# Part products stacked as 128 + 16 rows instead of 72 + 72, and the work around them put in another order, in the first of four attention-like layers

## The reference, cut to what matters

```
a = layer_norm(audio_kv)
Q, K, V = x @ Wq.T, a @ Wk.T, a @ Wv.T          # 16 heads of 16
scores  = where(mask, Q K^T / 4, -inf)
x       = x + tanh(gate) * (softmax(scores) V) @ Wo.T
```

## Time and profile before

| | |
|---|---|
| median of 3 timed runs | 1302.26 us |
| lowest and highest | 1301.91 and 1302.64 us |
| span of the profiled execution | 1301.2 us |
| mean granted clock of TensorE in it | 0.970 |
| instructions | 17916 |

### The profile page before, as it was taken

How to read it: one execution, slowest core, us unless ns; L and a number is a source line. 1 busy time by engine, 2 the same in 40 slices (tenths; PEclk the granted TensorE clock), 3 DMA queues, 4 the chain that set the end, 5 groups by cost and what they waited for, 6 DMA issues and landing times.

```text
span 1301.2 us, 17916 instructions
## 1 busy us (share of the span) xinstructions
PE 1222.6 (94%) x6064; PEld 859.9 (66%) x6064; DVE 792.9 (61%) x2354; ACT 537.2 (41%) x1233; POOL 216.2 (17%) x429
## 2 busy tenths in 40 slices
PE   6789989999998879999998899999999999999998
PEld 4467655556464434444433788888888888888887
DVE  4445438778675157787875666666656666666530
ACT  3145343444444315545555343434333434343432
POOL 3023025242434020112101100000000000000000
PEclk9689799999999879999999999999999999999999
DMA  7434741110202455515426903030303030500000
GB/s 226 141 114 136 222 155 64 57 64 35 81 26 93 135 177 183 159 73 164 139 83 198 312 1 130 1 130 1 130 1 130 1 131 1 195 1 1 1 9 25
DMA packets 100650, 127.58 MB, mean 98 GB/s; under 512 B 6736, under 2 KB 78576, under 8 KB 98320
## 3 DMA queue, kind: packets, MB, share of 16 engines
q1 hardware_dynamic: 99936, 126.14, 29.6%
q10 hardware_dynamic: 624, 0.30, 0.1%
HBM read 79.33 MB, written 46.79 MB: 97 GB/s over the span
## 4 chain that ended last, share of the span: by engine, by line
PE 79%; DMA 6%; DVE 4%; SPq 3%; ACT 3%; POOL 2%; issue 2%; ACTq 0%; POOLq 0%; DVEq 0%
PE J L2464 8%; PE J L2484 8%; PE TT L2472 8%; PE TT L2448 4%; PE S L2438 4%; PE OO L2438 4%; PE OO L1091 4%; PE OO L1088 4%; PE J L324 2%; PE J L1357 2%; PE OO L2705 2%; PE J L1091 2%; PE S L1327 2%; PE S L648 2%; PE J L333 2%
## 5 line engine op out<-in xcount | busy, mean ns | idle before, releaser
L2542 ACT ACTIVATE PT<-TT 128x512 f32<-128x512 f32 x128 | 76.4, 597 | 279.9 <-PE TT L2448 279.9
L2577 POOL COPY On<-probs 128x8 f32<-128x8 f32 x128 | 29.2, 228 | 470.0 <-DVE probs L2612 440.7
L2623 DVE TENSOR_SCALAR QK<-J,cols 128x256 f32<-128x256 f32 x126 | 61.0, 484 | 68.5 <-PE J L2464 68.5
L2612 DVE TENSOR_SCALAR probs<-probs,inv 128x257 f32<-128x257 f32 x256 | 79.0, 351 | 4.5
L2448 PE MATMUL TT<-ident,probs 128*128 128x128 f32 x512 | 76.9, 273 | 2.6 <-DVE probs L2612 2.6
L2448 PEld LDWEIGHTS TT<-ident,probs 128*128 128x128 f32 x512 | 63.8, 141 | 16.4 <-DVE probs L2612 3.8
L2618 DVE COPY km<-TT 128x256 f32<-128x256 f32 x128 | 54.2, 423 | 30.6 <-PE TT L2472 30.3
L1091 PE MATMUL OO<-ctxT,weights_a 128*128 128x512 f32 x136 | 66.4, 610 | 6.2 <-SPq L308 3.5
L1088 PE MATMUL OO<-weights_a,ctxT 128*128 128x512 f32 x136 | 65.9, 607 | 6.6 <-ACT weights_a L1102 3.4
L2331 DVE TENSOR_TENSOR_SCAN early<-km,early 128x256 f32<-128x256 f32 x64 | 64.3, 1044 | 10.9 <-ACT early L2102 10.1
L2484 PE MATMUL J<-early,km 128*128 128x256 f32 x256 | 65.8, 379 | 0.3 <-DVE km L2618 0.3
(11 more groups left out here) (414 smaller groups left out, 2711.7 us busy)
## 6 DMA issues: line engine op xcount, KB each, us to landing
wide_keys<-weights_a SPq DMA_DIRECT2D x64, 256.0 KB, 2.1
wide_values<-weights_a SPq DMA_DIRECT2D x56, 256.0 KB, 2.0
query_parts<-weights_a SPq DMA_DIRECT2D x48, 192.0 KB, 2.9
weights_a<-wide_keys SPq DMA_DIRECT2D x16, 512.0 KB, 7.3
weights_a<-wide_values SPq DMA_DIRECT2D x16, 512.0 KB, 8.4
early<-wide_keys SPq DMA_DIRECT2D x16, 512.0 KB, 7.8
early<-wide_values SPq DMA_DIRECT2D x16, 512.0 KB, 9.1
weights_a<-key_parts SPq DMA_DIRECT2D x16, 288.0 KB
```

Source lines behind the costliest of these rows:

```text
L2542: act.activation(PT[:, n % 2, :], T0[:, :], ACT.Copy).then_inc(pt3_ready, 1)
L2612: ins = dve.tensor_scalar(P_[n % 2][:, qt, :], P_[n % 2][:, qt, :], inv[:, qt, n % 32:n % 32 + 1], None, ALU.mult)
```

## The change

- The 144 rows lie as 128 + 16. Rows are ordered by query part `a`, feature, key part `c`: 48 rows for `a` = 0, 48 for `a` = 1, 32 for `a` = 2 with `c` below 2 fill the first tile; the 16 rows of the two lowest parts (`a` = `c` = 2) are the second tile, with the 3 rows of the maxima below them (`REST0`).
- A fill multiplies the first tile alone: two matmuls in place of four. The lowest part product is thus missing from the maxima, but not from the scores that the exponential sees: `transposed_scores` still uses both tiles.
- The queries are kept as two stores of 192 KB per batch, not six; both sides are repeated on reading. A step's rows now come in eight DMAs (48, 48, 32 and 16 rows for the keys, the same for the queries), each with the 16 features as outermost dimension of the source.
- The rows of steps 1 to 3 are asked for ahead of SP's loop; those of step n + 3 in step n, chunk 2. Batch 3 is prepared in step 1 (before in step 2), its statistics and root in step 0, and the values of batch 1 in step 0 (before in step 1).
- Ahead of the loop there is only unit 0; units 1 to 7 stand between the fills, at chunks -13, -11, -9, -7, -6, -5 and -3.

```diff
+        FEATS0 = 2 * HALF0
+        REST0 = FEATS0
+        TOPS0 = [PARTS, PARTS, PARTS - 1]
+        ROWS0 = [0, PARTS * FEATS0, 2 * PARTS * FEATS0]
...
+        FIRST_AT = [-13, -11, -9, -7, -6, -5, -3]
...
-            return n // 2 + 2 if n >= 0 and n % 2 == 0 and n // 2 + 2 < B else None
+            return n + 2 if 0 <= n < B - 2 else None
...
             for s in range(2):
-                for c in range(PARTS):
-                    sp.dma_start(query_parts0[b, s, :, c].rearrange("a p n -> p a n"),
-                                 parts0["q"][:, :, s * S:(s + 1) * S]).then_inc(query0_kept, 16)
+                sp.dma_start(query_parts0[b, :, s].rearrange("a p n -> p a n"),
+                             parts0["q"][:, :, s * S:(s + 1) * S]).then_inc(query0_kept, 16)
...
+        def feature_rows(parts, first):
+            return parts.rearrange("c s (d h) n -> (s d) c (h n)", d=HALF0)[:, :, first * S:(first + HEADS_AT) * S]
...
-            for s in range(2):
-                sp.dma_start(k_rows0[m % 4][0:ROWS0, s, :, :],
-                             key_parts0[b, s].rearrange("c (d h) n -> (c d) (h n)", d=HALF0)[:, here]
-                             .unsqueeze(0).to_broadcast([PARTS, PARTS * HALF0, n_here]))\
+            keys = feature_rows(key_parts0[b], first)
+            for a, top in enumerate(TOPS0):
+                sp.dma_start(k_rows0[m % 4][ROWS0[a]:ROWS0[a] + top * FEATS0, 0, :, :], keys[:, 0:top, :])\
                     .then_inc(rows0_landed[m % 4], 16)
+            sp.dma_start(k_rows0[m % 4][0:REST0, 1, :, :], keys[:, 2, :]).then_inc(rows0_landed[m % 4], 16)
...
+                sp.dma_start(q_rows0[m % 4][ROWS0[a]:ROWS0[a] + top * FEATS0, 0, :, :],
+                             queries[:, a:a + 1, :].to_broadcast([FEATS0, top, HEADS_AT * S]))\
...
             spread0(sp, 0)
+            keep_keys0(sp, 1)
             spread0(sp, 1)
-            keep_keys0(sp, 1)
             keep_queries0(sp, 1)
+            spread0(sp, 2)
+            spread0(sp, 3)
...
+                if 1 <= n <= STEPS0 - 4 and i == 2:
+                    spread0(sp, n + 3)
...
-                        for s in range(2):
-                            mm = pe.matmul((S0, S1)[n % 2][:, qt * S:(qt + 1) * S],
-                                           q_rows0[m % 4][0:ROWS0, s, f, qt * P:(qt + 1) * P],
-                                           k_rows0[m % 4][0:ROWS0, s, f, :], start=(s == 0), stop=(s == 1))
+                        mm = pe.matmul((S0, S1)[n % 2][:, qt * S:(qt + 1) * S],
+                                       q_rows0[m % 4][:, 0, f, qt * P:(qt + 1) * P],
+                                       k_rows0[m % 4][:, 0, f, :], start=True, stop=True)
...
-                            top = ROWS0 + (PARTS if s == 1 else 0)
+                            top = (P, REST0 + PARTS)[s]
...
-                for u in range(FIRST - 1):
...
+                first_unit(0)
...
                         if i == 0:
                             pe.wait_ge(max0_rows_ready, n + 1)
+                            if prepared(n - 1) is not None:
+                                pe.wait_ge(queries0_ready, following)
                             flip_x(following, O1)
...
-                    if i == 7 and n >= 0 and n % 2 == 1 and b + 1 < B:
+                    if i == 7 and n == 0:
+                        pe.wait_ge(h0_ready, 2)
+                        values(1, J0)
+                    if i == 7 and n >= 3 and n % 2 == 1 and b + 1 < B:
...
-                    if at == -1:
-                        u = FIRST + at
-                        pe.wait_ge(ahead_copied, u - 1)
-                        project_ahead(pe, (J1, O0)[u % 2], u)
+                    if at in FIRST_AT:
+                        first_unit(1 + FIRST_AT.index(at))
...
-                    if n in (-1, 1) and i == 0:
-                        root((n + 5) // 2 + 1)
+                    if n in (-1, 0) and i == 0:
+                        root(n + 4)
```

More of the change, by code:

```diff
@@ L514, in build @@
                   for n, i in (("q", 14336), ("k", 15104))}
-        key_parts0 = nc.dram_tensor("key_parts_0", [B, 2, PARTS, P, S], BF16).ap()
-        query_parts0 = nc.dram_tensor("query_parts_0", [B, 2, PARTS, PARTS, P, S], BF16).ap()
+        key_parts0 = nc.dram_tensor("key_parts_0", [B, PARTS, 2, P, S], BF16).ap()
+        query_parts0 = nc.dram_tensor("query_parts_0", [B, PARTS, 2, P, S], BF16).ap()
         RING0 = [T0, T1, O0]
+        FIRST_AT = [-13, -11, -9, -7, -6, -5, -3]
         def fill_of(at):
@@ L530, in keep_keys0 @@
             for s in range(2):
-                sp.dma_start(key_parts0[b, s].rearrange("c p n -> p c n"),
+                sp.dma_start(key_parts0[b, :, s].rearrange("c p n -> p c n"),
                              parts0["k"][:, :, s * S:(s + 1) * S]).then_inc(key0_kept, 16)
@@ L550, in spread_keys0 @@
                 sp.wait_ge(st0_done, CHUNKS0 * (m - 3))
-            here = slice(first * S, (first + HEADS_AT) * S)
-            n_here = HEADS_AT * S
             sp.wait_ge(key0_kept, 16 * 2 * (b + 1))
-            for s in range(2):
-                sp.dma_start(k_rows0[m % 4][0:ROWS0, s, :, :],
-                             key_parts0[b, s].rearrange("c (d h) n -> (c d) (h n)", d=HALF0)[:, here]
-                             .unsqueeze(0).to_broadcast([PARTS, PARTS * HALF0, n_here]))\
+            keys = feature_rows(key_parts0[b], first)
+            for a, top in enumerate(TOPS0):
+                sp.dma_start(k_rows0[m % 4][ROWS0[a]:ROWS0[a] + top * FEATS0, 0, :, :], keys[:, 0:top, :])\
                     .then_inc(rows0_landed[m % 4], 16)
+            sp.dma_start(k_rows0[m % 4][0:REST0, 1, :, :], keys[:, 2, :]).then_inc(rows0_landed[m % 4], 16)
         def spread_queries0(sp, m):
             b, first = m // 2, m % 2 * HEADS_AT
-            here = slice(first * S, (first + HEADS_AT) * S)
-            sp.wait_ge(query0_kept, 16 * 2 * PARTS * (b + 1))
-            for s in range(2):
-                sp.dma_start(q_rows0[m % 4][0:ROWS0, s, :, :],
-                             query_parts0[b, s].rearrange("a c (d h) n -> (a c d) (h n)", d=HALF0)[:, here])\
+            sp.wait_ge(query0_kept, 16 * 2 * (b + 1))
+            queries = feature_rows(query_parts0[b], first)
+            for a, top in enumerate(TOPS0):
+                sp.dma_start(q_rows0[m % 4][ROWS0[a]:ROWS0[a] + top * FEATS0, 0, :, :],
+                             queries[:, a:a + 1, :].to_broadcast([FEATS0, top, HEADS_AT * S]))\
                     .then_inc(rows0_landed[m % 4], 16)
+            sp.dma_start(q_rows0[m % 4][0:REST0, 1, :, :], queries[:, 2, :]).then_inc(rows0_landed[m % 4], 16)
         def split0(eng, n, ready, done_sem, turn, step_sem, at):
@@ L602, in stacked0_sp @@
                     store_first(sp, i)
[L603 to L613, removed]
+                if prepared(n) is not None and i == 4:
+                    keep_keys0(sp, prepared(n))
+                if prepared(n - 1) is not None and i == 1:
+                    keep_queries0(sp, prepared(n - 1))
+                if 1 <= n <= STEPS0 - 4 and i == 2:
+                    spread0(sp, n + 3)
                 if n == 4 and i == 2:
                     sp.wait_ge(key0_kept, 16 * 2 * B)
-                    sp.wait_ge(query0_kept, 16 * 2 * PARTS * B)
+                    sp.wait_ge(query0_kept, 16 * 2 * B)
                     load_values()
@@ L642, in fill @@
                     if f == 0:
-                        pe.wait_ge(rows0_landed[m % 4], 16 * 4 * (m // 4 + 1))
+                        pe.wait_ge(rows0_landed[m % 4], 16 * 8 * (m // 4 + 1))
                     if n >= 2:
@@ L726, in pe_program, with first_unit @@
                 pe.wait_ge(loaded["quarter"], 16)
-                for u in range(FIRST - 1):
+                def first_unit(u):
                     if u == 1:
@@ L771, in pe_program @@
                         if n == 1:
-                            pe.wait_ge(h0_ready, 2)
+                            pe.wait_ge(values0_ready, 2)
+                        elif n == 2:
+                            pe.wait_ge(ot0_ready, 1)
                         elif n % 2 == 1:
@@ L826, in fetch_queries @@
                         act.wait_ge(queries0_split, b)
-                        act.wait_ge(query0_kept, 16 * 2 * PARTS * b)
+                        act.wait_ge(query0_kept, 16 * 2 * b)
                     act.activation(exact0["q"], bank_[:, :], ACT.Copy, scale=DIM0 ** -0.5)
@@ L871, in act_program @@
                 act.wait_ge(mask_ready, 4)
-                for u in range(FIRST - 1):
-                    copy_first(act, (J1, O0)[u % 2], u)
+                copy_first(act, (J1, O0)[0], 0)
                 for at in range(-LEAD0, LAST0):
                     n, i = at // CHUNKS0, at % CHUNKS0
-                    if at == 0:
-                        copy_first(act, (J1, O0)[(FIRST + at - 1) % 2], FIRST + at - 1)
+                    if at - 1 in FIRST_AT:
+                        u = 1 + FIRST_AT.index(at - 1)
```

(11 more changed lines are left out.)

11 lines of the change are left out of this document (1 added, 10 removed).

## The result

The changed kernel takes 1284.34 us (median of four runs, 1283.18 to 1286.75) against 1302.45 (1301.91 to 1302.78) for the kernel before, measured beside it: a ratio of 0.9854, 95% interval [0.9825, 0.9884]. It is faster, and the time lies inside the range, but 18 us were gained where 38 were forecast. The profiled execution took 1286.75 us, its span 1284.9; 1.85 us lie around the span, where I had taken 1.0.

What follows compares the result with a forecast made beforehand. PE was taken as the bound from chunk 0, with waits and half clock. Of 37.9 us saved, 10.7 came from the head, 11.0 from matmuls, 10.6 from clock, 5.7 from waits: 1264 us, range 1254 to 1285.

Steps and rivals of the forecast that it cites:

- Part 1: Loop from chunk 0: 100 fill matmuls fewer at 0.11 us each, 11.0 us off, leaving 83.1 us; transposed scores unchanged.
- rival C: Head and loop: clock stays at half, partly because transposed scores use tiles of 16 or 19 rows; 1351 us, chance 0.03.
- the signs that I listed: New profile: first fill about 31, chunk 0 near 51, fills 0.22, DMA share near 1, clock 0.9 or more, end near 148.
- the signs of being wrong: First fill after 36, `L663` waiting on the maxima's DMA in several steps, or clock 0.5 for over some 20 us of loop.
- Part 2: Row spreads: features outermost bring them near the loads' pace, 3.6 us for a step's rows, against 15.1 at the old pace.
- Part 3: Head, step by step: first fill at 30.7 instead of 40.45 us, chunk 0 at 51 instead of 61.71, bounds 48 and 58.
- Part 4: Loop: 3 us of waits and 3 us for half clock added to 83.1 give 89.1; traffic costed at nothing.
- A: Loop: waits move to the maxima's DMA, 2.4 us more in each of four steps plus half clock; 1281 us, chance 0.18.
- D: Layer's end: the next layer's loads end last, near 166 instead of 148, so 18 of 38 us go; 1282, chance 0.04.
- the wait at 132.42: Loop wait on rows, forecast to go because their queries are projected a step earlier and six stores become two.
- The case of no change: Loop: DVE's maxima set the pace, so omitted matmuls leave idle time, and the head gains nothing; chance 0.02.
- The sum: Whole kernel: 51 + 89.1 = 140.1 in place of 178.04, 37.9 us less, span 1263.3, time 1264 us.

Runs made afterwards that it cites:

- e1: Changed kernel with the second tile of the transposed scores zero-padded and multiplied over all 128 rows; 1268.73 us, ratio 0.9719.
- e2: Changed kernel, 19 rows kept, tile order 128, 19, 19, 128, so two changes of height a chunk instead of four; 1272.65 us, ratio 0.9750.
- e3: As e1, but the zero-padded second tile is multiplied over 40 rows; 1285.78 us, ratio 0.9847.
- e4: As e1, but the zero-padded second tile is multiplied over 72 rows; 1266.92 us, ratio 0.9713.
- e5: e1 with each fill matmul issued twice, so a fill has four matmuls again; 1272.13 us, ratio 0.9748.
- e7: e1 with the copies, not the 16 features, as outermost dimension of the spreads' sources; 1294.30 us, ratio 0.9907.
- e8: e1 with the units' stores two steps earlier in SP's program and the 2 MB load two steps later; 1262.43 us, ratio 0.9692.
- e11: e8 with batch 3 prepared in step 2 again, its statistics staying in step 0; 1264.89 us, ratio 0.9718.
- e9: Changed kernel, 19 rows kept, with only e8's move of the units' stores and the 2 MB load; 1288.51 us, ratio 0.9877.

## Why the prediction was wrong

**Part 1** holds the step that failed: "The transposed scores keep their count of matmuls, so they change by nothing." The count stayed, but the change gave the two tiles of a sum the heights 128 and 19 where they had 72 and 75. Each change of height costs 0.10 us: 25.1 us in the loop, shown by e1 (gone with equal heights), e2 (half with half the changes) and e3 and e4 (which heights). So 83.1 us of work in the loop were forecast and 108.2 measured. I had costed matmuls by count and by columns, and had taken rows into account only for whether a matmul of 128 is dearer by itself and, in rival C, for the clock. That a matmul of 128 rows is not dearer by itself was right: it takes 0.11 us in e1 and e5. The fills paid too, 0.33 instead of 0.22 us, since each stands next to a tile of 19 rows; of the signs that I listed, the fill at 0.22 is one that failed in the loop, and none of the signs of being wrong watched the work itself.

**Part 2** was right. Features outermost bring the spreads to a share of 1.08, copies outermost take them back (e7, 25.6 us). The rule of the Trainium skill that I named beside it (DMA: Bandwidth & Descriptors, section Why a DMA increments its semaphore by 16 and not by 1) agrees with both forms: in e7 the shares of 0.19 and 0.13 are three and two of 16 engines, as many as the copies in its sources.

**Part 3** was right within 3 us. Two terms lie outside their bounds, both too long. For the rows of step 1 I had a wait of 0.7 to 2.5 us, and none came: the first fill of step 1 follows the unit before it at 39.16. For the maxima's DMA at chunk 0 I had at least 4.8 us, and from its issue at 44.12 to PE's go-on at 48.18 it took 4.06. The 2.17 us of wait there were followed by the only stretch at half clock in the loop, 6.8 us.

**Part 4**: waits and clock together came to 4.3 us in the changed kernel, where 6 were allowed. That was partly luck: slow scores gave the maxima time. Once the scores are fast, rivals A and D have a part in it, though not as I told them. Loads and stores do not end last; those issued close to a step's maxima are on the DMA engines while the maxima are on their way. e1 has 8.5 us of idle time in its loop and 5.1 of clock, and e8, with the same traffic at other times, 4.9 and nothing. I had costed the traffic at nothing. The reason that I gave for the wait at 132.42 was not borne out: with batch 3 back in step 2 (e11) it stays away. The stores, two instead of six, and the faster spreads are the parts of the change that are left for it; neither was tried by itself on the kernel before.

**Rivals**: C had half of the scores on small tiles and feared for the clock; the small tiles cost, but the clock did not fall. The case of no change, in which DVE sets the pace, did not come: DVE's 49.7 us stayed, and PE was busy for 111.57 of 112.52.

**The sum** comes out for a kernel that has equal heights and other times for its traffic: e8's loop is 88.83 us against 89.1, its time 1262.43 against 1264. Its waits and clock are split otherwise, 4.9 and 0 where I had 3 and 3.

## What to carry to other kernels

When a contraction is cut into tiles, count the changes of height between successive matmuls as well as the matmuls: with rows of zeros added to the small tile up to 72 or 128 the change is free here, and ordering tiles so that equal heights meet gets back half of the cost. Put in a DMA's outermost dimension something with many entries, not the three copies. And when a bound engine gets faster, look for the small transfer that it will wait for next: the work that is now gone had covered its landing. Moving bulk traffic away from it took most of those waits off (6 us by the medians, with overlapping intervals); look in the trace for where the traffic then lands, since the same move in e9 put it ahead of another such transfer.

## What the hardware showed that I had not expected

Each change between a matmul of 128 rows and one of 19 or 40 costs 0.10 us at 256 bf16 columns, almost a whole matmul (0.11); a change between 128 and 72 rows costs nothing. Adding work (zero rows) thus made the kernel 16 us faster.

The maxima's DMA always carries the same 24 x 256 maxima, but takes 4.06 us until PE goes on in the head, and 6.1 to 6.4 at two later waits in the loop (8.25 in e1). The windows between issue and go-on in the changed kernel, at chunk 0 and in two later steps:

```profile
44.12:48.18 4.06, 1.89 (x8) 0.80 (x7) 2.92 (x16) 0.60 (x1) 0.00 (x0) 1.00 0.89 213
118.08:124.48 6.40, 5.87 (x43) 3.22 (x42) 2.98 (x16) 2.96 (x5) 0.00 (x0) 1.00 1.00 348
132.20:138.34 6.14, 5.87 (x42) 3.21 (x42) 2.99 (x16) 2.96 (x5) 0.00 (x0) 1.00 1.05 343
```

The share is 0.89 to 1.05 in all three, but 213 GB/s move in the first and 343 and 348 in the others. e1 and e8 fit this, with 8.25 us at 338 GB/s and at most 4.46 at 218. Why it takes longer beside such traffic was not followed further.
